# A batch's GroupNorm and first convolution rows moved one loop earlier, its strips and its flag moved later

## What is computed

```
x = x + mix(groupnorm(x))                       # 4 batches, 128 channels, 32 x 32 pixels, float32
x = x + relu(deform_conv(groupnorm(x), offsets))
mix(g):   s = relu(cosine similarity of all pixel pairs) ** 2;  y = (g W0 + b0) summed with s over pixels
offsets = conv3x3(conv3x3(groupnorm(x), w1) + b1, w2) + b2        # 72 channels: 4 groups, 9 taps, (dy, dx)
deform_conv: each tap samples its group's 32 channels bilinearly at pixel + tap + offset, then 128 x 128 per tap
groupnorm: 32 groups of 4 channels, mean and variance over 4 x 32 x 32
```

## Time and profile before

| | us |
|---|---|
| median of three executions | 460.77 |
| lowest and highest | 460.49, 461.5 |
| the profiled execution | 459.05 |
| its span, first to last instruction | 457.0 |
| TensorE busy in the span | 405.2 (89%) |
| VectorE busy | 339.5 (74%) |
| ScalarE busy | 215.6 (47%) |
| mean granted TensorE clock | 0.97 of full speed |

### The profile page before, as it was taken

The page is one execution under the profiler, slowest core; times in us unless marked ns, Lnnn a source line. Parts: engine busy times, 40 slices in busy tenths (PEclk is TensorE's granted clock), DMA queues, the critical chain, the costliest instruction groups (busy, mean ns, idle before and its releaser), DMA issues.

```text
span 457.0 us, 9689 instructions
## 1 busy us (share of the span) xinstructions
PE 405.2 (89%) x3887; PEld 291.9 (64%) x3887; DVE 339.5 (74%) x586; ACT 215.6 (47%) x392; POOL 90.0 (20%) x99
## 2 busy tenths in 40 slices
PE   6698989979998789799999798989869898979996
PEld 6455557646665565678666575768556566857875
DVE  5995776829999999388854999376979945779901
ACT  3343254345555365441655446331845643257661
POOL 5444470001774100000546100000010000000000
PEclk9899999999999899999999899989979997999999
DMA  7200002250011124332001313442213243303330
GB/s 252 77 0 0 0 2 75 84 141 1 2 47 46 47 67 146 85 90 91 12 13 36 92 54 94 124 126 81 59 47 100 90 122 98 104 23 107 96 105 24
DMA packets 46157, 32.71 MB, mean 72 GB/s; under 512 B 3264, under 2 KB 43488, under 8 KB 46112
## 3 DMA queue, kind: packets, MB, share of 16 engines
q1 hardware_dynamic: 46048, 31.95, 23.5%
q10 hardware_dynamic: 64, 0.13, 0.1%
HBM read 25.24 MB, written 10.37 MB: 78 GB/s over the span
## 4 chain that ended last, share of the span: by engine, by line
PE 46%; DVE 32%; DMA 6%; SPq 5%; issue 4%; ACT 4%; POOL 1%; DVEq 0%; ACTq 0%; POOLq 0%
PE psB L788 10%; PE psB L555 9%; PE psT L739 7%; DVE wpix L1507 7%; PE psV L762 5%; DVE combo L1294 4%; PE psA L646 4%; DMA h_scr<-h_ring 3%; SPq L320 3%; DVE combo_p L1298 2%; DVE tent L1488 2%; PE psA L555 2%; DVE tent L1482 2%; PE psB L813 2%; PE psA L813 2%
## 5 line engine op out<-in xcount | busy, mean ns | idle before, releaser
L1021 ACT ACTIVATE wcell<-psT 128x512 f32<-128x512 f32 (+1 forms) x160 | 83.9, 552 | 70.2 <-PE psT L739 68.9
L1507 DVE TENSOR_TENSOR wpix<-tent 128x512 f32<-128x512 f32 (+1 forms) x160 | 99.7, 675 | 14.4 <-PE psT L739 13.3
L739 PE MATMUL psT<-ident,wpix 128*128 128x128 f32 x576 | 89.1, 288 | 12.4 <-ACT wcell L1021 12.0
L739 PEld LDWEIGHTS psT<-ident,wpix 128*128 128x128 f32 x576 | 68.8, 148 | 37.2 <-issue 29.5
L493 POOL TENSOR_TENSOR sim<-rel 128x512 f32<-128x512 f32 x48 | 61.4, 1299 | 69.0 <-ACT rel L978 69.0
L1045 ACT ACTIVATE val<-psV 128x576 f32<-128x576 f32 x64 | 44.0, 688 | 30.7 <-PE psV L762 30.2
L788 PE MATMUL psB<-val,wd_sb 128*128 128x256 f32 x216 | 51.2, 392 | 0.0
L762 PE MATMUL psV<-wcell,hwin 64*32 64x144 f32 x2048 | 47.2, 294 | 3.9 <-ACT val L1045 3.5
L646 PE MATMUL psA<-sim,scratch 128*128 128x512 f32 x96 | 45.6, 597 | 0.6 <-POOL sim L493 0.6
L788 PEld LDWEIGHTS psB<-val,wd_sb 128*128 128x128 f32 x216 | 40.7, 193 | 8.3 <-issue 2.9
L555 PE MATMUL psB<-g_p 128*128 128x512 f32 x144 | 40.9, 419 | 0.0
(11 more groups left out here) (193 smaller groups left out, 453.6 us busy)
## 6 DMA issues: line engine op xcount, KB each, us to landing
hwin<-h_scr SPq DMA_DIRECT2D x128, 128.0 KB, 2.9
h_scr<-h_ring SPq DMA_DIRECT2D x8, 576.0 KB
h_ring<-sim SPq DMA_DIRECT2D x4, 512.0 KB
x_all<-x SPq DMA_DIRECT2D x1, 1536.0 KB, 10.0
out<-yout SPq DMA_DIRECT2D x12, 128.0 KB, 1.8
off_scr<-sim SPq DMA_DIRECT2D x4, 288.0 KB
combo<-sim SPq DMA_DIRECT2D x32, 32.0 KB
val<-w SPq DMA_DIRECT2D x1, 576.0 KB, 6.1
```

Of the source, the lines that this page charges most:

```text
L739: last = pe.transpose(bank[:, at:at + P], wpix[:, t % 2, k, 2 * h:2 * h + 2, :].rearrange("p g q -> p (g q)"), ident[:, :])
L1021: act.activation(wcell[:, t % 2, taps[0]:taps[-1] + 1, :, :].rearrange("q k h p -> q (k h p)"), bank[:, 0:len(taps) * G // 2 * P], ACT.Cop ...
L1507: dve.tensor_tensor(w, ty, tx, ALU.mult).then_inc(s["weights_done"], 1)
```

## The change

Only batch 3 (`FIRST_AHEAD`) gets another schedule; SP's order changes for all.

- GroupNorm of batch 3 goes from slots 23 to 28 of loop 2 to slots 57 to 60 of loop 1 (`AHEAD`), with its moments in two free columns of `psB`.
- The four combines, high and low parts of its first convolution go from slots 29 to 33 of loop 2 into the tail of loop 1 (`ROWS_AHEAD`, steps -8 to -1): in VectorE's queue the first two combines ahead of `add_out(1, 0)`, the others between the weights of tile 1; in ScalarE's one high part ahead of `relu_out(1, 0)`, one ahead of each `take_samples` of tile 7, one behind.
- In loop 2 (`SPREAD_OUT`) the first convolution takes slots 4 to 17, its output rows 18; the second has its rows in 18 to 24, products in 26 to 40, output rows in 41, wrap in 42; the turn of the offsets 56 and 58; the image 22. `shift_offsets(3)` goes ahead of `windows(2, 6)`.
- In loop 2 the weights of tiles 5 to 7 go to the slots in which TensorE turns those two tiles earlier (`W_EVEN`), and those of tile 0 of batch 3 to slot 60.
- `lay_image(b+1)` goes behind `windows(b, 7)`.
- The extremes of batch 3 go to slot 24 of loop 3 with the first half of `find_farthest`, the turn to slot 42, the rest (`set_flag`) to slot 46.

```diff
+        ROWS_AHEAD = ((-8, -8, -5, -3), (-6, -4, -2, -1), (-8, -7, -4, -2))
+        SPREAD_OUT = dict(combine=[ROWS_AHEAD[0], (18, 18, 21, 23)], low=[ROWS_AHEAD[1], (20, 21, 23, 24)],
+                          high=[ROWS_AHEAD[2], (19, 20, 22, 24)], conv=[(4, 7, 8, 13, 16, 17), (26, 29, 31, 34, 35, 40)],
+                          copy=[9, 32], sums=[16, 36], rows=[18, 41], mean=None, dev=None, var=None, norm=None, flat=2,
+                          image=22, wrap=42, shift=None, turn={56: (0, 1), 58: (2, 3)}, extremes=None)
+        AHEAD = dict(mean=57, dev=57, var=59, norm=60)
+        W_EVEN = {t: tuple(K * (t - 2) + k for k in TURN_SLOT) for t in range(2, ROWT)}
+        LEAD_WEIGHTS, FIRST_WEIGHTS, LAST_WEIGHTS, LEAD_EXTREMES = 60, 67, 60, 12
+        FIRST_AHEAD = 3
+        LAST_EXTREMES, LAST_FARTHEST, LAST_FLAG = 24, 42, 46
...
                 for t in range(2, ROWT):
-                    if t == IMAGE_TILE and b + 1 < B:
+                    image, shifts = (5, 6) if b + 1 == LAST else (5, 7)
+                    if t == image and b + 1 < B:
                         store_image(b + 1)
-                    if t == IMAGE_TILE + 1 and b + 1 < B:
-                        lay_image(b + 1)
-                    if t == ROWT - 1 and b + 1 < B:
+                    if t == shifts and b + 1 < B:
                         shift_offsets(b + 1)
...
                 else:
+                    lay_image(b + 1)
                     for t in range(2):
                         windows(b + 1, t)
...
+                    if m == 1 and FIRST_AHEAD <= b + 2 < B:
+                        pe.wait_ge(s["sd_done"], b + 3)
...
+                def rows_ahead(lo, hi):
+                    if FIRST_AHEAD <= b + 2 < B:
+                        for step in range(lo, hi):
+                            conv_front(b + 2, step, front(b + 2))
+
+                rows_ahead(-8, -7)
                 relu_out(b, 0)
+                rows_ahead(-7, -6)
                 take_samples(b, ROWT - 1, 0)
+                rows_ahead(-6, -3)
                 take_samples(b, ROWT - 1, 1)
+                rows_ahead(-3, 0)
                 for m in range(1, 4):
                     relu_out(b, m)
...
+                        if b == LAST and n == LAST_EXTREMES:
+                            find_extremes(LAST)
+                            find_farthest()
+                        if b == LAST and n == LAST_FLAG:
+                            set_flag()
...
+                rows_ahead(-8)
                 add_out(b, 0)
-                if nxt is not None:
-                    for i in range(len(TAPS)):
-                        weights(nxt, 1, i)
+                for i in range(len(TAPS)):
+                    weights(nxt, 1, i)
+                    rows_ahead(i - 6)
+                rows_ahead(-1)
                 for m in range(1, 4):
                     add_out(b, m)
```

## The result

The changed kernel takes **470.95 us** (median of 4 runs, 468.04 to 472.2), beside 461.05 us of the kernel before, timed with it: a ratio of 1.021, 95% interval 1.017 to 1.025. It is slower, and within a microsecond of the forecast of 470.4. Its profiled execution, the fastest of the four, took 468.04 us with a span of 466.2, against 459.05 and 457.0.

A forecast was written before the change was run, and what follows sets the result against it. The prediction took a chain of waits, mostly TensorE and VectorE, as the bound. Tail +8.1, loop 2 -4.2 and loop 3 +5.7 gave +9.6 us: 468.65 us profiled, 470.4 us as median, range 460.0 to 476.

The forecast's parts named there:

- The tail of loop 1: End of loop 1: high copies queued ahead of relus and samples delay TensorE's last sample product and third deform step; +8.1 us.
- Rival (2): Tail of loop 1: rows ready in time, only VectorE's surplus paid, at most 2.0 us; total 457.9 us; chance 0.14.
- GroupNorm in loop 1: Slots 57 to 60 of loop 1: batch 3's GroupNorm costs between 0 and 0.5 us there, taken as 0.
- Loop 2: Loop 2: same matmul work, 65.9 us, with new stalls; 79.0 against 83.2 us, so -4.2 us.
- slot 26: Second convolution's start in loop 2: TensorE stalls 2.0 us on VectorE, then a slow stretch costs 1.7 us more.
- slot 56: Offsets' turn in loop 2: TensorE stalls 4.9 us, then a slow stretch costs 3.3 us.
- Loop 3: Loop 3: wait at its head gone, -1.35, flag stall +5.3, slow stretch +1.7; +5.7 us in all.
- The 5.3 us of the flag: Slot 50 of loop 3: fifth deform group waits 5.2 to 5.3 us for far_all_done, 2.4 with VectorE on time.
- Strips laid last: SP's queue: 0 to 0.5 us in loops 0 and 1; VectorE 3.4 us behind TensorE at loop 3's start.
- rival (4): End of loop 2: strips land early, VectorE only 0.8 us behind TensorE, flag 2.6 us earlier; 467.8 us; chance 0.05.
- Rival (1): All loops: TensorE stays at 2.4 GHz, no new slow stretches; +2.4 us, 463.2 us; chance 0.28.
- Rival (3): Whole kernel: moves cancel, stalls replace one another, tail near 5 us; within a microsecond of 460.8; chance 0.06.

The follow-up runs named there:

- samples_first: Changed kernel with another order in ScalarE's tail of loop 1: relu_out(1, 0) and both take_samples first, then the high copies; 464.44 us, ratio 1.011.
- the last kernel: Changed kernel with samples first, add_out(1, 1) earlier, offsets' turn later, flag early, strips still last, and two stores ahead of the windows; 450.71 us, ratio 0.977.
- the second profile: Profile of the changed kernel timed once more, unaltered; 469.84 us, ratio 1.022.
- changed_stores_first: Changed kernel with the first two stores of a loop ahead of the eight windows; 467.13 us, ratio 1.015.
- strips_last_only: The kernel before with one move alone, lay_image(b+1) behind windows(b, 7) in all loops; 467.11 us, ratio 1.015.
- strips_early: Changed kernel with lay_image(b+1) back ahead of windows(b, 6), the offsets' shift right behind it; 473.64 us, ratio 1.029.
- the four parts that help: Changed kernel with one edit each: samples ahead of high copies, turn five slots later, flag early, two stores first; 464.44, 464.82, 467.29, 467.13 us.
- strips_last_stores_first: The kernel before with strips laid behind windows 7 and the first two stores ahead of the eight windows; 460.18 us, ratio 1.000.
- all_undone_holds: Changed kernel with samples first, add_out(1, 1) earlier, offsets' turn later, flag early, and strips ahead of windows 6; 460.30 us, ratio 1.001.

## Why the prediction was right, and where it was not

**The tail of loop 1** went by the mechanism given, step by step. Loop 0 ends 2.3 us later in this profile; with that taken off, the two first combines end at 311.9 (311.6 forecast), the last sample product starts at 313.4 (313.2) after 4.33 us (4.1), and the third deform step at 318.6 (318.4). Loop 1 is 7.6 us longer (8.1): 5.4 us more without a matmul (12.59 less 7.22) and 2.2 more of matmuls (97.24 less 95.05), most of it in the slow stretch of the tail (0.60 over 4.3 us). `samples_first` shows that the order of ScalarE's queue is the cause. Rival (2), in which only VectorE's surplus of 2.0 us is paid, fell; with the order of `samples_first` the tail comes near it, 0.6 us in loop 1 and 2.66 at the head of loop 2. These 0.6 us leave little for GroupNorm in loop 1 (0 to 0.5 forecast), which no run tried alone.

**Loop 2** was forecast 1.7 us too long; the clock terms of the sum were mis-sized. At slot 26 I had a stall of 2.0 us with 1.7 us of slow clock; it was 1.03 us, with 1.18 on ScalarE's copy just ahead that I had not listed. No slow stretch followed in this profile. One followed in the second, and loop 2 is as long there, 77.4 us: 1.45 us more of matmuls and 1.3 less of idle time. So the slow stretch ran into time that was idle otherwise, and the forecast was wrong to add it whole. At slot 56 the stall was 4.26 for 4.9 us, and 4.38 us of matmuls ran at 0.50, which costs half of that, 2.2, where I had 3.3. So slow matmuls cost 2.2 us and not 5.0, the work is 67.44 - 2.2 = 65.2 by this estimate (65.9 forecast; the last kernel's loop 2, at the full clock, has 65.83), and the idle time is 9.9 us (7.9 with its terms added up): small waits that I had not listed, of 0.3 to 0.7 us on copies and windows, make the rest.

**Loop 3** was right in its parts. VectorE began 3.8 us behind TensorE (3.4). The 5.3 us of the flag came as 1.44 + 3.46 = 4.9 us, in two waits because TensorE catches up with VectorE's weights before it reaches slot 50. The slow matmuls cost 48.10 - 46.44 = 1.66 us (1.7), and nothing in the second profile, where loop 3 is 4.0 us longer than before. The sentence that the wait would be 2.4 us with VectorE on time was tested: 2.22 in `changed_stores_first`. There loop 3 was still 2.8 us longer than before. The forecast said that TensorE works on from slot 50 without a gap worth naming; there is one of 0.93 us, at 444.13, but the changed kernel has it too (0.94), so it moves nothing.

**Strips laid last** is the step that failed in its reasoning, though not in the sum. I had 0 to 0.5 us for loops 0 and 1, because `add_out` would be late by some tenths at most. In the changed kernel that holds at the end of loop 1, where the third sum waits for ScalarE (325.49), but only since the tail is late anyway: in `strips_last_only` the same move idles VectorE for 7.23 us there and costs 6.3 us in all. And I priced the strips and the earlier offsets apart. `strips_early` shows that they belong together: without the move of the strips, TensorE gets the offsets 7 us later. The strips at the end of loop 2 took 13.9 us from their issue to the first window behind them (387.22 to 401.12; 14.4 forecast), so rival (4), which needed under 12, fell. Its price for VectorE on time was right (467.8; 467.13 measured), but two stores ahead of the windows brought it, not a quicker transfer.

**Rival (1)**, the clock holds, fell: three of the waits are followed by windows at 0.50 to 0.66, and only the last of them is missing in the second profile. Rival (3) needed a tail near 5 us, which was 7.6.

**The start.** The 2.3 us up to the end of loop 0 were not forecast. Most of them are there before the change can act: SP issues batch 0's strips, ahead of the first loop, at 77.01 us where the kernel before has 75.32, and up to there every engine runs the same instructions in the same order. In the other profiles this issue lies between 74.7 and 79.1 us. The end of loop 0 lies there at 217.5 and 219.4 us with the strips early and between 216.9 and 221.4 with the strips last; the scatter is as large as the difference, so I don't put it down to the change. Without these 2.3 us the stages give +7.1, against a sum of +9.6. The closeness of the total is thus partly an accident: loops 1 to 3 were forecast 2.5 us too long in all, and the start made up for it.

**Do the single parts add up?** Against the first median of the changed kernel the four parts that help give -6.5, -6.1, -3.7 and -3.8 us, 20.1 in all, and the last kernel -20.2. But these medians come from different groups. Taken above the kernel before of each group, the changed kernel stands at +9.9 us (+9.35 the second time) and the parts at +3.7, +4.1, +6.5 and +7.5, which gives back 17.9, and the last kernel 18.8. So the agreement of 20.1 and 20.2 shows nothing: the edits for flag and stores overlap in the same wait, and the last kernel has one more edit, `add_out` earlier, that was not tried alone.

## What to carry to other kernels

An operation moved ahead is paid not by its duration but by what stands behind it in the queue of each engine that takes part: here a 0.66 us copy held finished samples for 6 us, and windows that waited for a transfer held the stores of buffers that VectorE wanted. When a transfer is moved on a shared queue, look at what used to be in front of it and at what is now behind it, for the next user of that queue may only work because of the move. Before giving up a change that is slower, undo its side effects one at a time; here the moves, with the order around them mended, were worth 2.3%, while the two stores first brought the kernel before nothing (`strips_last_stores_first`).

## What the runs showed of the hardware

- Slow stretches do not follow from the length of a wait. In one profile of the changed kernel the granted clock is 1.00 in the 5.4 us behind waits of 1.18 and 1.03 us, in the other 0.69. Behind 3.46 us on the flag it is 0.66 over 3.7 us in the one, behind 3.47 us 1.00 in the other. After 4.26 us it was 0.50 for 4.4 us, and after 2.67 us in `strips_last_only` 0.57 over 8 us. In the ten profiles with the spread loop 2, the 3.3 us behind the wait at slot 26 (1.03 us in each) have a clock of 0.50 to 0.60 in seven and of 1.00 in three.
- Nine transfers of 32 KB that TensorE can use 8.1 us after their first issue take 15.0 us with a 1.18 MB DRAM copy just ahead of them on the queue (15.6 in `all_undone_holds`), although the DMA engines' busy share is 0.54 in that time (371.1 to 386.0 in `strips_early`).
- Executions of one kernel differ by more than a per cent here: 466.39 to 472.2 us in the eight runs of the changed kernel, with a mean granted clock of 0.942 to 0.967, and 457.5 to 462.5 in those of the kernel before that the ratios use. The 95% intervals of the ratios reach 0.3 to 0.6% to either side, more than the 0.2% that the prediction took for what can be told from no change.
